# Thirty 128x1792 low-half subtractions moved from GpSimd to VectorE in the feed-forward stage of a gated block

## What is computed

```python
x = x + tanh(g_xattn) * attention(layernorm(x), ctx, ctx, w_q, w_k, w_v)   # causal, 512 wide
n = layernorm(x)
h = gelu(n @ ternary(W1).T + b1)        # 2048 wide, ternary weights -1, 0, 1
x = x + tanh(g_ffn) * (h @ ternary(W2).T + b2)
```

## Time and profile before

| what | value |
|---|---|
| median of three runs | 1629.68 us (1628.36 to 1630.47) |
| the profiled execution | 1629.08 us, of it span 1627.3 us |
| mean granted clock of TensorE | 0.994 |
| PE busy | 1573.7 us, 97% of the span, 10028 instructions |
| VectorE (DVE) busy | 1048.8 us, 64% |
| ACT busy | 808.6 us, 50% |
| GpSimd (POOL) busy | 534.9 us, 33% |
| feed-forward stage | from about 757 us to the end, 64 units |

### The profile page before, as it was taken

How to read it: one execution, slowest core, us unless ns; L and a number is a source line. 1 busy time by engine, 2 the same in 40 slices (tenths; PEclk the granted TensorE clock), 3 DMA queues, 4 the chain that set the end, 5 groups by cost and what they waited for, 6 DMA issues and landing times.

```text
span 1627.3 us, 26067 instructions
## 1 busy us (share of the span) xinstructions
PE 1573.7 (97%) x10028; PEld 979.7 (60%) x10028; DVE 1048.8 (64%) x1795; ACT 808.6 (50%) x1448; POOL 534.9 (33%) x497
## 2 busy tenths in 40 slices
PE   7799999999999999989999999999999999999998
PEld 4455556565656555555666666666666666666665
DVE  6656667575656688875666556655665566656644
ACT  2333333323333542324665666566666666666664
POOL 3211111111111111142554455345634464445420
PEclk9899999999999999999999999999999999999999
DMA  6445454443647896664333133213322242223120
GB/s 207 110 96 149 104 140 107 133 118 91 154 97 192 202 255 165 154 149 95 78 89 84 29 92 98 75 49 73 98 75 62 59 98 75 75 46 98 50 50 26
DMA packets 307532, 170.81 MB, mean 105 GB/s; under 512 B 268160, under 2 KB 268176, under 8 KB 306128
## 3 DMA queue, kind: packets, MB, share of 16 engines
q1 hardware_dynamic: 306512, 166.78, 41.8%
q10 hardware_dynamic: 720, 2.10, 0.4%
q0 software_dynamic: 176, 0.27, 0.1%
HBM read 70.53 MB, written 33.55 MB: 64 GB/s over the span
## 4 chain that ended last, share of the span: by engine, by line
PE 81%; DVE 10%; issue 2%; ACT 2%; SPq 1%; POOL 0%; DMA 0%; DVEq 0%
PE s_ps L1227 11%; PE e_ps L1227 11%; PE s_ps L1292 11%; PE o_ps L1322 10%; PE v_ps L1273 8%; PE t_ps L1254 8%; PE v_ps L1171 7%; PE t_ps L1171 6%; PE o_ps L1171 6%; DVE v_s L1041 4%; PE m_ps L1171 3%; ACT xnT L664 1%; DVE w_s L1071 1%; DVE tT L1035 1%; DVE bn L999 1%
## 5 line engine op out<-in xcount | busy, mean ns | idle before, releaser
L1041 DVE SCALAR_TENSOR_TENSOR v_s<-xnT,sc,v_s 128x512 f16<-128x512 f32 x256 | 263.5, 1050 | 104.9 <-ACT v_s L671 104.9
L664 ACT ACTIVATE xnT<-tT,b_s 128x256 f32<-128x256 f32 x384 | 173.9, 500 | 220.4 <-DVE tT L1035 105.2
L1227 PE MATMUL e_ps<-w_s,v_s 128*128 128x512 f16 x1024 | 262.8, 379 | 0.0
L1227 PE MATMUL s_ps<-w_s,v_s 128*128 128x512 f16 x1024 | 262.8, 379 | 0.0
L567 ACT ACTIVATE p<-s_ps,ebias,esc 128x128 f32<-128x128 f32 (+3 forms) x64 | 53.2, 831 | 355.4 <-DVE ebias L905 355.4
L1292 PE MATMUL s_ps<-ctx_s,tT 128*128 128x512 f16 (+3 forms) x1152 | 197.8, 326 | 3.4 <-DVE tT L862 3.4
L1322 PE MATMUL o_ps<-v_s,pT 128*128 128x512 f16 x840 | 191.6, 379 | 0.0
L1273 PE MATMUL v_ps<-wv_s,ctx_s 128*128 128x512 f16 x768 | 178.7, 383 | 8.9 <-DVE v_s L869 8.9
L1254 PE MATMUL t_ps<-xnT,a_s 128*128 128x256 f16 x1488 | 176.9, 276 | 8.8 <-issue 8.6
L671 ACT ACTIVATE v_s<-xnT,sc 128x512 f16<-128x512 f32 x256 | 176.2, 712 | 7.5
L1227 PEld LDWEIGHTS e_ps<-w_s,v_s 128*128 128x128 f16 x1024 | 100.2, 98 | 120.8
(11 more groups left out here) (168 smaller groups left out, 2388.1 us busy)
## 6 DMA issues: line engine op xcount, KB each, us to landing
out_y<-x_ring SPq DMA_DIRECT2D x128, 256.0 KB, 2.1
x_ring<-in_x SPq DMA_DIRECT2D x64, 256.0 KB, 2.9
raw<-in_ctxT SPq DMA_DIRECT2D x7, 2048.0 KB, 8.3
raw<-out_y SPq DMA_DIRECT2D x44, 256.0 KB, 3.7
w_in<-in_w1T SPq DMA_DIRECT2D x16, 512.0 KB, 4.6
w_in<-in_w2T SPq DMA_DIRECT2D x16, 512.0 KB, 4.6
x_ring<-out_y SPq DMA_DIRECT2D x20, 256.0 KB, 3.9
raw<-in_ctxT SPq DMA_DIRECT2D x2, 1024.0 KB, 16.5
```

The lines of the kernel that those rows point to most:

```text
L664: a.activation(g32n[:, j, half * 2 * P:(half + 1) * 2 * P], src, ACT.Gelu, bias=b1_s[:, f:f + 1], scale=1.0 / YN).then_inc(g_act, 1)
L1041: v.scalar_tensor_tensor(out=g_s[:, U % 2, j, LO], in0=g32n[:, j], scalar=col(C_SG), in1=g_s[:, U % 2, j, HI], op0=ALU.mult, op1=ALU.subtr ...
L1227: last_mm = mm(y_ps[i], g_s[:, U % 2, j, a, i * P:(i + 1) * P], w2_s[:, f, :], start=(U % UG == 0 and n == 0 and a == HI), stop=(U % UG == ...
```

## The change

In the unit loop GpSimd no longer calls `y_lower`. VectorE gets a `y_lower` of its own, with the same operands, wait and semaphore, and calls it as the last thing of its list for the unit, behind both `y_normal`. The units in which it is called (U - 1 in `ROWS_Q0` or `ROWS_Q1`) stay the same, and so do the two calls of the last attention slots, on GpSimd. That is 30 instructions, two for each of the groups 1 to 15.

```diff
             last_sum(0)
             for U in range(NU):
-                if U - 1 in ROWS_Q0:
-                    y_lower(2 * ROWS_Q0[U - 1])
-                if U - 1 in ROWS_Q1:
-                    y_lower(2 * ROWS_Q1[U - 1] + 1)
                 if U in ROWS_Q0:
...
+            def y_lower(q):
+
+                r8, r7 = rows_at(q)
+                dve.wait_ge(y_hi, q + 1)
+                v.tensor_tensor(r7[:, LO].rearrange("p o n -> p (o n)"), r8[:, 1:8].rearrange("p o n -> p (o n)"),
+                                r7[:, HI].rearrange("p o n -> p (o n)"), ALU.subtract).then_inc(y_lo, 1)
...
                     y_normal(q0 * GT + 1)
                 if q1 is not None:
                     y_normal(q1 * GT + 3)
+                if U - 1 in ROWS_Q0:
+                    y_lower(2 * ROWS_Q0[U - 1])
+                if U - 1 in ROWS_Q1:
+                    y_lower(2 * ROWS_Q1[U - 1] + 1)
             finish_rows(NG - 1)
```

## The result

The changed kernel takes 1616.26 us, the median of five runs (1613.35 to 1617.04), against 1630.23 us for the kernel before (1628.36 to 1631.23, five runs). The ratio is 0.9911, with a 95% interval of 0.9897 to 0.9924. The profiled execution has a span of 1614.5 us, where it was 1627.3.

The account below looks back on a forecast made before the run. The prediction took the feed-forward stage to be bound by PE (TensorE). Its terms, 1629.1 - 22.0 + 5.9 + 2.6 = 1615.6 us, with the median 0.6 higher, gave 1616 us, range 1611 to 1625.

Parts of the forecast that it names:

- What bounds the stage: Feed-forward stage: PE hardly waits, so only what shortens or adds a PE wait counts; undisturbed units last 13.02 us.
- Minus 22.0 us: Taking first-half subtractions off GpSimd removes 15 PE waits on ACT's line 691, 1.47 us each with restart.
- The subtraction on VectorE: Each of 30 moved 128x1792 subtractions takes 2.03 us, scaled from line 919; upper bound 3.59 us.
- End of A: Units with U % 4 = 0: first-half subtraction delays y_sums; line 685 keeps 1.37 us spare, cost nothing.
- End of B: Units with U % 4 = 1: second-half subtraction, held by one line 489, ends 13.44 us in; cost nothing.
- The transposes: Group 1's second half comes later, so PE waits 7.5 us ahead of unit_first(4): plus 5.9 us, once.
- rival 1: The wait ahead of unit_first(4) has another cause and does not grow: 1607.1 us, chance 0.05.
- The clock: After the long wait ahead of unit_first(4) PE runs at half clock: plus 2.6 us, bounds 0 to 3.4.
- The rule weighed: Whether GpSimd holds a VectorE tensor_tensor with two SBUF inputs: held 1615.6 us, not held 1614.5.
- Rivals 2 to 4: New stall per group, 1619 to 1628, 0.15; y_sums delay reaches PE, 1643.5, 0.07; old stall stays, 1637.6, 0.03.
- slack of 1.34 us: Inside a unit, VectorE's line 1035 can come this much late before PE loses time: 2.81 late cost 1.47.
- rival 3: Holding y_sums delays ACT and passes to PE in full, 1.86 us in 15 units: 1643.5 us, chance 0.07.

Follow-up runs that it names:

- e2_second_halves: Against the kernel before, only the second halves' subtractions move to VectorE, the first halves stay on GpSimd; 1638.70 us, ratio 1.0050.
- e1_first_halves: Against the kernel before, only the first halves' subtractions move to VectorE, the second halves stay on GpSimd; 1609.28 us, ratio 0.9870.
- e3_split_pool: Kernel before with nothing moved; GpSimd's subtraction of 1792 columns is issued as two of 896; 1607.00 us, ratio 0.9860.
- e4_double_first: Changed kernel, with VectorE making each first-half subtraction twice, first into an unused buffer; 1635.94 us, ratio 1.0036 to the kernel before.
- e5_bias_later: Changed kernel, with GpSimd's four bias additions (line 489) one unit later; 1615.77 us, ratio 0.9915 to the kernel before.
- e8_early: Changed kernel, with group 1's second-half subtraction ahead of unit_second in VectorE's list for unit 2; 1608.21 us, ratio 0.9869 to the kernel before.
- e6_fill: Changed kernel, with 32 unread TensorE products ahead of the wait in unit_first(4); 1613.75 us, ratio 0.9906 to the kernel before.

## Why the prediction was right, by its own steps

**What bounds the stage.** Right. PE's waits, and the clock behind one of them, were the whole account: the stage went from 869.92 to 855.61, 14.3 us, and the terms as measured, 15 x 1.47 = 22.0 off, 5.9 and 1.8 on, give 14.3. The runs' medians moved by 14.0. That the time itself, 1616.26, lies within 0.3 us of the 1616 written is in part luck: the fall written was 13.5, 0.5 to 0.8 short, and it was taken from a median of three runs (1629.68), where the median of five is 1630.23.

**Minus 22.0 us.** Right in size and cause. e2_second_halves keeps all 15 waits, e1_first_halves has none of them, and e3_split_pool takes them away with the work left on GpSimd, so it is the length of one GpSimd instruction between two of VectorE's.

**The subtraction on VectorE.** 2.03 us from line 919, measured 2.01.

**End of A.** The subtraction started at 10.79 us into A, as written. The sums ended at 1060.07, 2.55 into B (2.6 written), line 681 at 1063.07, 5.55 in (5.57), and line 1031 started 5.66 in (5.60). PE lost nothing. e4_double_first shows where the room ends.

**End of B.** It asked at 10.33 and ended at 1070.94, 13.42 in (13.44). VectorE's pair in C ended at 4.97 (near 5.0).

**The transposes.** Wait 7.47 us, 7.5 written; 6.19 us from subtraction to PE. e5_bias_later and e8_early move the subtraction and the wait follows, to 6.40 and 0.99 us, so rival 1 (another cause for that wait) falls. It was the largest cost of the change, and it sits at one unit of 64.

**The clock.** The term that was mis-sized: 2.6 written, 1.8 measured (e6_fill: 1.8; the two units around that wait last 9.4 us more than two undisturbed ones, 7.6 for the wait with its restart and 1.8 for the clock). I took the time at half clock after an idle stretch from one other place. Half of it was the right rule, but the time differs from run to run: the same sum of two units gives 1.3 us in e5_bias_later and 1.9 in e2_second_halves. It lay within the bounds of 0 to 3.4.

**The rule weighed.** The subtraction of B is held, 3.09 against 2.01 us, so the sum with the hold was the right one.

**Rivals 2 to 4.** Apart from the wait ahead of `unit_first(4)` and the clock behind it no unit of a group is above 13.02 us, so there was no new stall. The slack of 1.34 us on which this rested measured 1.35. The holding of `y_sums`, rival 3, does happen (2.44 us for L471), and the delay reaches ACT, but stays inside the room. It takes a second subtraction to turn it into a loss.

## What to carry to other kernels

When an engine that is not the bound has one instruction several times its usual length, look at what ran on the other of VectorE and GpSimd at that moment: here 22 of 1630 us hung on 15 GpSimd instructions of 3.6 us of work, each between two short ones of VectorE. Cutting it in two was enough here and left every other order as it was; moving it also moves its result, and then the first pass through a loop, where the lead is shortest, has to be looked at by itself. One group out of fifteen had a unit less of lead, and took back 7.7 us of the 22.

## What the runs showed of the hardware

GpSimd's issued next instruction does not keep VectorE out: in e3_split_pool VectorE's held one went ahead of GpSimd's second piece, recorded as begun 0.04 us before the first ended. A VectorE instruction with a single tensor in SBUF can be held too: the tensor_scalar of line 1015 takes 1.49 us in each of the 15 disturbed units of the kernel before, where it comes just behind GpSimd's line 495, and 0.54 us where line 495 comes behind it:

```profile
1053.59 1.29 POOL L495 TENSOR_TENSOR tT<-tT 128x512 f32<-128x512 f32 x1 [0.54 <-ACT tT L691]
1053.67 1.49 DVE L1015 TENSOR_SCALAR v_s<-raw,mv,rstd 128x512 f32<-128x512 f32 x1
```

A wait of 7.47 us ahead of `unit_first(4)` brought TensorE from 2.4 to 1.2 GHz from 817.2 to 824.0 us, of which PE had work for 3.64 us; the waits of 0.99 and 2.0 us at the same place (e8_early, e1_first_halves) brought no fall there.
